# A macaron layer on one core: normalized rows turned by VectorE in squares and moved by DMA, in place of transposes on TensorE

## The reference

```
x = x + 0.5 * ffn(layernorm(x))
x = x + attention(layernorm(x))
x = x + 0.5 * ffn(layernorm(x))
```

## Time and profile before

| | |
|---|---|
| median of 3 runs (lowest, highest) | 1857.75 us (1857.65, 1857.84) |
| the profiled execution's own time | 1859.35 us |
| its span, first to last instruction | 1857.6 us |
| TensorE busy, granted clock | 1837.3 us (99%), 0.999 |
| VectorE, ScalarE, GpSimd busy | 841.1, 525.6, 140.5 us |
| DMA queues of SyncE, ScalarE, GpSimd, share of 16 engines | 40.3%, 9.3%, 7.7% |

### The profile page before, as it was taken

How to read it: one execution, slowest core, us unless ns; L and a number is a source line. 1 busy time by engine, 2 the same in 40 slices (tenths; PEclk the granted TensorE clock), 3 DMA queues, 4 the chain that set the end, 5 groups by cost and what they waited for, 6 DMA issues and landing times.

```text
span 1857.6 us, 22348 instructions
## 1 busy us (share of the span) xinstructions
PE 1837.3 (99%) x8608; PEld 1529.7 (82%) x8608; DVE 841.1 (45%) x1599; ACT 525.6 (28%) x802; POOL 140.5 (8%) x246
## 2 busy tenths in 40 slices
PE   7999999999999999999999999999999999999999
PEld 5888888888888888888888888888888888888887
DVE  7557453555345563324433556344654324422222
ACT  3324322532124432112212533124532111311111
POOL 1131110100000000000010010000100000000000
PEclk9999999999999999999999999999999999999999
DMA  5986755445455455476655555455455466657664
GB/s 193 384 304 241 265 189 179 161 171 173 148 193 183 160 171 177 134 260 213 224 183 183 177 193 171 160 192 177 156 170 175 146 223 217 210 174 241 220 238 170
DMA packets 90345, 366.83 MB, mean 197 GB/s; under 512 B 11680, under 2 KB 12064, under 8 KB 69504
## 3 DMA queue, kind: packets, MB, share of 16 engines
q1 hardware_dynamic: 50064, 262.89, 40.3%
q10 hardware_dynamic: 27792, 47.20, 9.3%
q0 software_dynamic: 12384, 55.32, 7.7%
HBM read 323.55 MB, written 41.81 MB: 197 GB/s over the span
## 4 chain that ended last, share of the span: by engine, by line
PE 94%; DVE 3%; ACT 1%; issue 1%; DMA 0%; SPq 0%; ACTq 0%; DVEq 0%
PE bank L1057 27%; PE bank L1059 27%; PE bank L1058 27%; PE bank L1270 4%; PE bank L1067 1%; PE bank L1211 1%; PE bank L1203 1%; PE bank L1210 1%; PE bank L1197 1%; PE bank L1255 1%; PE bank L1256 0%; PE bank L1087 0%; PE bank L1088 0%; PE bank L1095 0%; DVE act_t L677 0%
## 5 line engine op out<-in xcount | busy, mean ns | idle before, releaser
L1057 PE MATMUL bank<-x_hi,wt 128*128 128x512 f32 x1328 | 524.0, 395 | 0.0
L1059 PE MATMUL bank<-x_lo,wt 128*128 128x512 f32 x1328 | 517.8, 390 | 0.0
L1058 PE MATMUL bank<-x_hi,wt 128*128 128x512 f32 x1328 | 517.0, 389 | 0.0
L677 DVE TENSOR_TENSOR act_t<-bank,sig 128x512 f32<-128x512 f32 x176 | 121.6, 691 | 568.9 <-PE bank L1270 511.7
L1059 PEld LDWEIGHTS bank<-x_lo,wt 128*128 128x128 f32 x1328 | 249.2, 188 | 53.2
L1058 PEld LDWEIGHTS bank<-x_hi,wt 128*128 128x128 f32 x1328 | 249.6, 188 | 50.2
L1057 PEld LDWEIGHTS bank<-x_hi,wt 128*128 128x128 f32 x1328 | 249.5, 188 | 49.5
L1057 PE MATMUL bank<-dt,a_hi 128*128 128x512 f32 x704 | 279.1, 396 | 0.3 <-DVE a_lo L677 0.3
L1059 PE MATMUL bank<-dt,a_hi 128*128 128x512 f32 x704 | 274.8, 390 | 0.0
L1058 PE MATMUL bank<-dt,a_lo 128*128 128x512 f32 x704 | 274.4, 390 | 0.0
L601 ACT ACTIVATE sig<-bank 128x512 f32<-128x512 f32 x176 | 105.5, 599 | 526.7 <-PE bank L1270 526.6
(11 more groups left out here) (178 smaller groups left out, 1684.0 us busy)
## 6 DMA issues: line engine op xcount, KB each, us to landing
wt<-scr_w SPq DMA_DIRECT2D x140, 1152.0 KB, 5.2
dt<-scr_d SPq DMA_DIRECT2D x140, 512.0 KB, 5.2
s_bc<-scr_s ACTq DMA_DIRECT2D x128, 256.0 KB, 5.1
state<-wat POOLq DMA_DIRECT2D x28, 512.0 KB, 6.4
scr_w<-wt POOLq DMA_DIRECT2D x12, 1024.0 KB, 7.9
b_all<-wgu SPq DMA_DIRECT2D x22, 512.0 KB, 7.9
scr_d<-dt POOLq DMA_DIRECT2D x22, 512.0 KB, 4.0
scr_w<-tw POOLq DMA_DIRECT2D x10, 1024.0 KB, 7.7
```

Of the source, the lines that this page charges most:

```text
L677: return nc.vector.tensor_tensor(dst, a, b, op)
L1057: mm(dst, wh, xh, start=start, stop=False)
L1058: mm(dst, wl, xh, start=False, stop=False)
L1059: return mm(dst, wh, xl, start=False, stop=stop)
```

## The change

After the first LayerNorm, TensorE turns no normalized rows. Behind each `norm`, VectorE transposes the tile in blocks of 32x32 (`turn_squares`) into `squares`, which lies in `tb`. When four tiles are done, 16 transfers of 32 partitions with 2 KB each (64 KB) put the blocks in place, eight issued by SyncE and eight by GpSimd (`move_squares`). They land in `x_lo`; ScalarE rounds from there into `x_hi`, 1024 columns at a time, and VectorE subtracts in place, in two instructions where there were four. A tile now is 32 tokens of each quarter of a block: the host permutes x and the output so, `x_hi`, `x_lo` and `a_hi`, `a_lo` have their columns in another order, and the matmuls with x moving read four runs of 128 columns.

Norms and squares of a router come in slots 30 and 31 (31 and 32 where the phase has attention), rounding and rest in 36 and 37, the logits stay in 38; of attention's in slots 5 and 6, 10 and 11, and 13. `move_squares` stands on SyncE behind `load_w` of chunk 12 (4 for attention), on GpSimd behind `rstd_of` for a router (behind the load of the second slab for attention). In phase 0 it is at c == 12 on SyncE and c == 10, behind `store_d`, on GpSimd. The gated output is turned in slots 61 and 63, four transposes each, rounded by two instructions each, kept in the slab buffer that is free (`ogT`), and projected in slots 64 and 65 into two banks in turn.

The core of the diff (indentation cut by eight; sizes, the gated output on ScalarE and VectorE, and the host's permutation left out):

```diff
--- before.py
+++ after.py
@@ -76,12 +78,14 @@
 x_res = sb("x_res", [P, 3, NT, D])
-x_hi = sb("x_hi", [P, 2, KC, NB], F32R)
-x_lo = sb("x_lo", [P, 2, KC, NB], F32R)
+
+x_hi = sb("x_hi", [P, 2, NQ, KC, NT, Q], F32R)
+x_lo = sb("x_lo", [P, 2, NQ, KC, NT, Q], F32R)
 softT = sb("softT", [P, 2, 2, NB], F32R)
 s_bc = sb("s_bc", [P, 2, NB])
-a_hi = sb("a_hi", [P, 2, NB], F32R)
-a_lo = sb("a_lo", [P, 2, NB], F32R)
+
+a_hi = sb("a_hi", [P, 2, NT, NQ, Q], F32R)
+a_lo = sb("a_lo", [P, 2, NT, NQ, Q], F32R)
 scal = sb("scal", [P, NT, G])
@@ -139,6 +143,8 @@
 xn = o_all[:].rearrange("p (a b) c -> p a (b c)", a=2)
+
+squares = tb[:, 0:4, :].rearrange("p j (k i t) -> p j k i t", k=KC, i=NT)
 tb_flat = tb[:].rearrange("p a b -> p (a b)")
@@ -218,8 +233,19 @@
 
-def tr_bank(p, i):
-    return YB[i] if p == 0 else W1
+def turned(s):
+
+    return x_lo[:, s, :, :, :, :].bitcast(F32)
+
+def by_quarter(a):
+
+    return a.rearrange("p i b t -> p b i t")
+
+def in_order(a):
+    return a.rearrange("p (b i t) -> p b i t", b=NQ, i=NT)
+
+def norm_slot(p):
+    return 31 if p - 1 in ATT else 30
 
@@ -280,6 +306,13 @@
 
+    def move_squares(r, s):
+
+        sp.wait_ge(sq_ok, r * NT)
+        for b in range(0, 2):
+            for j in range(NQ):
+                sp.dma_start(turned(s)[cols(j, Q), b, :, :, :], squares[cols(b, Q), j, :, :, :]).then_inc(sq_in[0], 16)
+
     for i in range(NT):
@@ -301,8 +336,12 @@
                 load_w(p, c)
+            if c == 4 and p in ATT:
+                move_squares(LN_T[ATT[p]], (p + 1) % 2)
             if c > 2:
                 load_d(p, c - 1)
+            if c == 12 and p + 1 < PHASES:
+                move_squares(LN_R[p + 1], (p + 1) % 2)
             if p == 3 and c == 6:
@@ -328,6 +367,12 @@
 
+    def move_squares(r, s):
+        pool.wait_ge(sq_ok, r * NT)
+        for b in range(2, NQ):
+            for j in range(NQ):
+                pool.dma_start(turned(s)[cols(j, Q), b, :, :, :], squares[cols(b, Q), j, :, :, :]).then_inc(sq_in[1], 16)
+
     def store_w(c):
@@ -458,20 +506,19 @@
 
-    def hi(r, i, s, b):
-        act.wait_ge(xT_ok, r * NT + i + 1)
-        copy(x_hi[:, s, :, cols(i)], b[:].rearrange("p (k c) -> p k c", k=KC)).then_inc(x_hi_ok, 1)
+    def first_hi(i):
+        act.wait_ge(xT_ok, i + 1)
+        copy(x_hi[:, 0, :, :, i, :], YB[i][:].rearrange("p (k b t) -> p b k t", k=KC, b=NQ)).then_inc(x_hi_ok, 1)
+
+    def hi(r, m, s):
+        act.wait_ge(sq_in[m], 16 * 2 * NQ * r)
+        b = slice(2 * m, 2 * m + 2)
+        copy(x_hi[:, s, b, :, :, :], turned(s)[:, b, :, :, :]).then_inc(x_hi_ok, 2)
 
...
         r = LN_R[p]
-        if k in (32, 33, 35, 36):
-            i = (32, 33, 35, 36).index(k)
-            if i == 0 and p:
-
-                wait(act, u_ok, (p - 1) * CH)
-                if p - 1 in ATT:
-                    act.wait_ge(k_mm, (ATT[p - 1] + 1) * H)
-            hi(r, i, p % 2, tr_bank(p, i))
+        if k in (36, 37) and p:
+            hi(r, k - 36, p % 2)
         elif k == 38:
@@ -726,14 +771,27 @@
         dve.wait_ge(rstd_ok, r * NT + i + 1)
-        wait(dve, xT_ok, r * NT + i - 1)
+        if r == 0:
+            wait(dve, xT_ok, i - 1)
         nc.vector.tensor_scalar(xn[:, i % 2, :], src[:, i, :], mv[:, i, 0:1], rstd[:, i:i + 1],
...
 
-    def low(r, i, s, b):
-        dve.wait_ge(x_hi_ok, r * NT + i + 1)
-        tt(x_lo[:, s, :, cols(i)], b[:].rearrange("p (k c) -> p k c", k=KC),
-           x_hi[:, s, :, cols(i)].bitcast(F32), ALU.subtract).then_inc(x_lo_ok, 1)
+    def turn_squares(r, i):
+        dve.wait_ge(xn_ok, r * NT + i + 1)
+        nc.vector.transpose(squares[:, :, :, i, :].rearrange("p j k t -> p k j t"),
+                            xn[:, i % 2, :].rearrange("p (k j t) -> p k j t", k=KC, j=NQ)).then_inc(sq_ok, 1)
+        dve.wait_ge(sq_ok, (r - 1) * NT + i + 1)
+
+    def first_low(i):
+        dve.wait_ge(x_hi_ok, i + 1)
+        tt(x_lo[:, 0, :, :, i, :], YB[i][:].rearrange("p (k b t) -> p b k t", k=KC, b=NQ),
+           x_hi[:, 0, :, :, i, :].bitcast(F32), ALU.subtract).then_inc(x_lo_ok, 1)
+
+    def low(r, m, s):
+        dve.wait_ge(x_hi_ok, r * NT + 2 * m + 2)
+        b = slice(2 * m, 2 * m + 2)
+        tt(x_lo[:, s, b, :, :, :], turned(s)[:, b, :, :, :], x_hi[:, s, b, :, :, :].bitcast(F32),
+           ALU.subtract).then_inc(x_lo_ok, 2)
 
@@ -741,24 +799,28 @@
         stt = nc.vector.scalar_tensor_tensor
-        if k == 28:
+        if k == 27:
             if not FINAL[p]:
...
             stats_of(r, 1, src)
-        elif k == 29:
+        elif k == 28:
             stats_of(r, 2, src)
             stats_of(r, 3, src)
-        elif k == 31:
-            norm(r, 0, src)
-            norm(r, 1, src)
-        elif k in (32, 33, 35, 36):
-            i = (32, 33, 35, 36).index(k)
-            low(r, i, p % 2, tr_bank(p, i))
-            if i < 2:
-                norm(r, i + 2, src)
+        if k in (norm_slot(p), norm_slot(p) + 1):
+            i = 2 * (k - norm_slot(p))
+            if i == 0:
+
+                wait(dve, u_ok, (p - 1) * CH)
+                if p - 1 in ATT:
+                    dve.wait_ge(k_mm, (ATT[p - 1] + 1) * H)
+            for j in (i, i + 1):
+                norm(r, j, src)
+                turn_squares(r, j)
+        elif k in (36, 37):
+            low(r, k - 36, p % 2)
         elif k == 39:
@@ -872,14 +934,16 @@
 
-            wait(dve, ogT_ok, t * NT)
-            norm(r, 0, xb)
-            norm(r, 1, xb)
-        elif k in (7, 8, 10, 11):
-            i = (7, 8, 10, 11).index(k)
-            low(r, i, s, (W0, W1)[i % 2])
-            if i < 2:
-                norm(r, i + 2, xb)
+            wait(dve, ogT_ok, 2 * t)
+
+            dve.wait_ge(u_ok, q * CH)
+            dve.wait_ge(routeT_ok, 2 * (q + 1))
+        if k in (5, 6):
+            for i in (2 * k - 10, 2 * k - 9):
+                norm(r, i, xb)
+                turn_squares(r, i)
+        if k in (10, 11):
+            low(r, k - 10, s)
         if k in (13, 14, 15, 16):
@@ -1058,34 +1124,33 @@
 
-    def xk(s, k, c=slice(0, NB)):
-        return x_hi[:, s, k, c], x_lo[:, s, k, c]
-
-    def turn(r, i, b):
-        pe.wait_ge(xn_ok, r * NT + i + 1)
+    def xk(s, k):
+        return tuple(x[:, s, :, k, :, :].rearrange("p b i t -> p b (i t)") for x in (x_hi, x_lo))
+
+    def xtile(s, k, b):
+        return tuple(x[:, s, b, k, :, :].rearrange("p i t -> p (i t)") for x in (x_hi, x_lo))
+
+    def first_turn(i):
+        pe.wait_ge(xn_ok, i + 1)
         for k in range(KC):
-            ins = nc.tensor.transpose(b[:, cols(k)], xn[:, i % 2, cols(k)], ident[:])
+            ins = nc.tensor.transpose(YB[i][:, cols(k)], xn[:, i % 2, cols(k)], ident[:])
         ins.then_inc(xT_ok, 1)
...
         r, s = LN_R[p], p % 2
-        if k in (32, 33, 35, 36):
-            i = (32, 33, 35, 36).index(k)
-            if i == 0 and p:
+        if k == 38:
+            if p:
 
...
                 done = sum(q < p - 1 for q in ATT)
-                wait(pe, og_lo_ok, done * NT)
+                wait(pe, x2_ok, done * NT)
                 if p - 1 in ATT:
                     pe.wait_ge(q_cp, (ATT[p - 1] + 1) * H)
-            elif p:
-                pe.wait_ge(x_lo_ok, r * NT + i)
-            turn(r, i, tr_bank(p, i))
-        elif k == 38:
             pe.wait_ge(x_lo_ok, (r + 1) * NT)
             for kk in range(KC):
-                mm(W1[:], gate_s[:, kk, :], x_hi[:, s, kk, :], start=(kk == 0), stop=False)
-                ins = mm(W1[:], gate_s[:, kk, :], x_lo[:, s, kk, :], start=False, stop=(kk == KC - 1))
+                hi, lo = xk(s, kk)
+                mm(W1[:], gate_s[:, kk, :], hi, start=(kk == 0), stop=False)
+                ins = mm(W1[:], gate_s[:, kk, :], lo, start=False, stop=(kk == KC - 1))
             ins.then_inc(logit_ok, 1)
@@ -1122,38 +1187,31 @@
 
-        if k in (7, 8, 10, 11):
-            i = (7, 8, 10, 11).index(k)
+        if k in (13, 14, 15, 16):
+            i = k - 13
             if i == 0:
+                pe.wait_ge(x_lo_ok, (r + 1) * NT)
 
...
                     pe.wait_ge(m_raw_ok, CH)
-            elif i == 1:
-                pe.wait_ge(route_cp, 2 * (q + 1))
-                wait(pe, og_lo_ok, t * NT)
             else:
-                pe.wait_ge(x_lo_ok, r * NT + i - 1)
-            turn(r, i, (W0, W1)[i % 2])
-        if k in (13, 14, 15, 16):
-            i = k - 13
-            if i == 0:
-                pe.wait_ge(x_lo_ok, r * NT + 3)
-            else:
-                pe.wait_ge(x_lo_ok, r * NT + 4)
                 pe.wait_ge(gt_ok, t * NT + i)
...
                 hi, lo = slab(S_VG + kk // 2)
-                ins = three(W0[:], xk(s, kk, cols(i)), (hi[:, kk % 2, :], lo[:, kk % 2, :]), kk == 0, kk == KC - 1)
+                ins = three(W0[:], xtile(s, kk, i), (hi[:, kk % 2, :], lo[:, kk % 2, :]), kk == 0, kk == KC - 1)
             ins.then_inc(vg_mm, 1)
         if k == 14:
-            pe.wait_ge(x_lo_ok, r * NT + 4)
+
+            pe.wait_ge(route_cp, 2 * (q + 1))
```

(90 more changed lines are left out.)

44 lines of the change are left out of this document (24 added, 20 removed).

## The result

The changed kernel took 1840.6 us in the median of four runs (1837.8 to 1843.6), beside 1857.8 for the kernel before on the same chip: a ratio of 0.9906, 95% interval [0.9888, 0.9923], faster by 17 us. Forecast was 1837.0, with 1834 to 1846 as the range. The profiled execution took 1840.9 us, its span 1839.1; that of before took 1859.35 and 1857.6, so the span lost 18.5 us where the sum said 20.8.

What follows compares the result with a forecast made beforehand. TensorE, busy 1837.3 of 1857.6 us, was taken to bound the kernel. 21.0 us removed less 0.2 added gave 20.8, so the median 1857.75 would become 1837.0, with a range of 1834 to 1846.

Steps and rivals of the forecast that it cites:

- (d): Rival, slots 31 to 33: busier VectorE sets the pace, nothing moves; 0.05, shared with other cases just eating the gain.
- (b): Rival, squares' transfers: each queue serves them one behind the other, median 1861.5 or about 2080; chance 0.05.
- (a): Rival, LayerNorms: squares come partly late, 0.5 to 1 us on each of 11, giving 1842 to 1848; chance 0.11.
- What goes: On TensorE: 44 turns of four transposes, 18.2 us, and the waits in front of them, 2.75; together 21.0 us.
- The turns behind wide matmuls: On TensorE: 32 turns at 0.435 us each, including 0.085 for the first matmul after an fp32 operation, 13.9 us.
- The 12 behind other fp32 work: TensorE, attention phases: 12 turns directly behind other fp32 work, 0.36 us each as the 0.085 extra stays, 4.3 us.
- the gated output's grouping: On TensorE: 32 transposes in eight visits of four instead of sixteen of two, 3.6 against 3.5 us: nothing.
- What comes: Before the logits without attention: TensorE waits 0.1 us for the second rest, twice, 0.2 us; all else fits.
- In phase 0 the masked weights' matmuls give it 1 us more.: Router of phase 0: the second rest before the logits has 1 us more time, so no wait there.
- A landing ... I take 4.6, so 391.5 ... need 9.1.: Router in an attention phase: squares ready at 382.4 land by 391.5, needing 9.1 us where 13.3 are allowed.
- More room for the transfers: Routers without attention (phases 0, 3, 6): norms one slot earlier, so transfers have more room; no size given.
- 15 us of room after taking off a rounding and a rest: Attention's norms, second phase: squares ready at about 265.5, first use at 284.90 less 1.7, leaving 15 us.

Runs made afterwards that it cites:

- turns: The changed kernel with the 44 turns back on TensorE in their old slots, no squares and no moves: 1859.3 us, ratio 0.9998 to the kernel before.
- nomove: The changed kernel without the 16 transfers, squares rounded where VectorE wrote them, so x is mixed up: 1837.1 us, ratio 0.9878 to the kernel before.
- early: The changed kernel with norms, transfers and roundings sooner in phases 0, 3 and 6, roundings by two slots: 1834.9 us, ratio 0.9876 to the kernel before.
- 1835.3: The early kernel with attention's moves ahead of SyncE's weight load of the same chunk: 1835.3 us, ratio 0.9869 to the kernel before.
- 1857.1 us: The early kernel with all 16 transfers of a LayerNorm on GpSimd's queue: 1857.1 us, ratio 0.9988 to the kernel before.

## Why the prediction was right, and where it was off

**The mechanism held.** TensorE was the bound, its turns were its own time, and their going was paid out: turns (nothing) and nomove (0.9878) enclose it. VectorE's 31 us of turning cost nothing; (d) is out, as is (b): landings overlap (5.5 us in the median with eight and eight in a row). (a), the squares partly late, is what happened at a small size: at three places, not eleven.

The accounts below go by the starts of the softT matmuls, two in each chunk of both kernels: where the difference between after and before steps, something has gone or come.

**What goes: forecast 21.0, it was 25.2.** The turns behind wide matmuls were priced at 0.435 and are worth 0.49. One of them, from the last matmul ahead of it to the softT behind it, before and after:

```profile
850.79 0.39 PE L1059 MATMUL bank<-dt,a_hi 128*128 128x512 f32 x1
...
854.23 0.39 PE L1270 MATMUL bank<-softT,wt 128*128 128x512 f32 x1
```
```profile
843.39 0.39 PE L1125 MATMUL bank<-dt,a_hi 128*128 128x512 f32 x1
...
846.34 0.39 PE L1329 MATMUL bank<-softT,wt 128*128 128x512 f32 x1
```

3.44 us against 2.95. The turn and the matmul behind it hold 0.44 of that; the other 0.04 to 0.05 are in the ten matmuls after, which start 0.231 apart where 0.227 is usual. Over 32 turns that is 1.6 us. The 12 behind other fp32 work were priced at their own start to the next matmul, 0.36. Before, where the third one was:

```profile
380.40 1.05 PE L1203 MATMUL bank<-vtz,k2t 128*128 128x128 f32 x8
381.29 0.60 PE L1067 MATMUL bank<-ident,o_all 128*128 128x128 f32 x4
381.65 0.48 PE L1057 MATMUL bank<-x_hi,wt 128*128 128x512 f32 x1
```

and after:

```profile
378.52 1.05 PE L1261 MATMUL bank<-vtz,k2t 128*128 128x128 f32 x8
379.32 0.48 PE L1123 MATMUL bank<-x_hi,wt 128*128 128x512 f32 x1
```

From the eight to the next wide matmul were 1.25 us and are 0.80: 0.45, not 0.36, because the eight themselves take 0.89 ahead of a turn and 0.80 ahead of a wide matmul. Eight turns were short by 0.08 each, 0.7 us. In the four with a wait it is 377.34 - 375.44 = 1.90 before and, as the next fence shows, 0.81 after: 1.09 where turn and wait stood at 0.82. The idle time of 0.46 is counted from the modelled end of the eight, at 376.49, not from where the next could have started.

```profile
374.64 1.05 PE L1255 MATMUL bank<-q_all,b_all 128*128 128x128 f32 x8
375.45 0.48 PE L1123 MATMUL bank<-x_hi,wt 128*128 128x512 f32 x1
```

Four times 0.27 is 1.1 us, and the fifth wait, in phase 0, adds 0.3 likewise. With the 1.6 above, the turns and their waits are worth 24.7 instead of 21.0, and the gated output's grouping, put at nothing, gave 0.55. A price read as the distance between two matmuls well ahead of and behind the instruction, with it and without, would have given the turns' part before the run.

**What comes: forecast 0.2, it was 6.7.** Waits of 4.0; 0.2 to 0.3 more with each of the three, as idle time counts from the modelled end of the matmul before, 0.39 after its start, where the next would have started 0.23 after it, and the first matmul behind a wait holds the next one back by 0.1; 1.6 of slower clock behind the first (below); and 0.3 in phase 6, where the forecast said 0.1 and the mechanism was the one that it named. Four steps failed:
- "In phase 0 the masked weights' matmuls give it 1 us more." The opposite: their preparation (the gate's product on VectorE, two roundings on ScalarE) stands in the same line in front of the second rest. 1.9 us, shown by nomove and gone in early.
- "A landing ... I take 4.6, so 391.5 ... need 9.1." It held where it was worked out, in the routers of attention phases (8.5 to 9.1), but it was not worked out for the others, and there it was too short. In phase 3 SyncE issued its last transfer 4.7 us after the squares were ready (its issues took 0.58 in the mean, not 0.32), and that one took 7.4 us to land, where the sum had 4.5 for GpSimd's issuing and 4.6 for the landing. The medians of the landings, 5.4 and 4.8 us, are near the forecast, but what is waited for is the last. In the attention of phase 2 it was 13.4 (519.1 to 532.5).
- "More room for the transfers" without attention: in phase 3 ScalarE wanted the squares at 856.0, 10.9 us after they were ready, less than the 13.3 of an attention phase. That figure I had not worked out, only asserted. 12.2 - 10.9 = 1.3 is nearly the whole wait of 1.36.
- "15 us of room after taking off a rounding and a rest" for attention's norms: between landing and first product stand two roundings and two rests with a chunk's rounding and rest of a in between, 4.2 us (532.58 to 536.71 in phase 2) and not 2.3. The room was 13.1 us, and with 13.4 to landing TensorE waited.

**The sum.** 25.2 - 6.7 = 18.5, as by the spans. That the forecast came within 4 us of the median owes something to luck: what goes was put 4.2 us too low and what comes 6.5 too low, and the two errors have opposite signs in the sum.

## What to carry to other kernels

- Where one engine has no idle time, a small operation is worth moving off it, even to a slower path of three steps, provided the path's latency is summed with the real issue times of each queue and the landing of the last transfer, and compared with the room at each place separately.
- In front of a queue of large loads, the order of issue counts: send first what is needed first, on as many queues as issue it quickly, and let the loads stand behind. The sum of bytes was the same in 1835.3 and in 1857.1 us, though the two differ in the issuing queue as well.
- Price a removed instruction as the distance between two matmuls around it less the same distance without it, taken from another place of the same trace, and take the second a dozen matmuls behind; the instruction's own row misses what its neighbours pay.
